# Third expert layer: the three low-rank products of a hidden bank stacked into one of 96 rows, and the first chunk's whole-rank products placed ahead of the low-rank inputs

## The chip, the cores and the metric

The kernel runs on one core of one Trainium2 chip. The metric is the device time of one execution in microseconds; lower is better. Three runs of a kernel give its median.

## The reference, cut to what matters

The model is four pairs of a cross-attention layer and an expert layer over 2048 tokens (8 batches of 256) of 256 features. Only the third expert layer is touched. It is one shared network of 1024 hidden units plus, for each token, a low-rank term of the one expert that the token's gate ranks first:

```
gate   = softmax(y @ gate_W.T + gate_b)           # 8 experts
chosen = one_hot(argmax(gate))                    # one expert a token
u      = y @ lora_A.T, kept for the chosen expert # 8 experts x 4 ranks = 32 columns
hidden = relu(y @ wi.T + wi_b + u @ lora_B)       # 1024 hidden units
x      = x + tanh(g) * (hidden @ wo.T + wo_b)     # y is the normalised x
```

## The kernel before, in words

Everything is one program with one instruction list an engine. The layers follow each other, with all engines meeting at their borders. In the third expert layer (function `experts`, and `choose_low_rank` for the gate) the hidden units are two units of 512 (index `u`), and the tokens four chunks of 512 (index `c`).

Each operand of a product is split into a high part (a rounding copy on ScalarE, helper `high`) and a low part (the rest, a subtraction on VectorE, helper `low`). A product of two operands is then three products on TensorE: high by high, high by low, low by high.

The function `first(u, c)` on TensorE makes the hidden numbers of a chunk in four PSUM banks of 128 hidden units by 512 tokens. For each bank it issues nine products of 512 columns: six whole-rank ones (two halves of the 256 features, three terms each, over 128 partitions) and three low-rank ones over 32 partitions (`lbh` by `uh`, `lbh` by `ul`, `lbl` by `uh`). ScalarE then reads each finished bank twice with the bias and the relu (a whole copy, L1380, and a rounded one, L1381) and counts the semaphore `activated`; VectorE makes the low part (L1386, `f_hl`). The function `second(u, c)` multiplies back in 48 products of 256 columns (L1339), and VectorE adds the four results to the residual (L1412). `run_ahead` sets the order on TensorE and VectorE: `first(0, 0)`, and then `first` of the next chunk always ahead of `second` of this one.

Before all this the low-rank inputs are made. VectorE computes the gate's softmax and the first largest (L1023 to L1045), masks the 32 low-rank columns (`um`, L1238), TensorE turns them chunk by chunk (`turn_inputs`, L1303, two PSUM banks by turns), ScalarE copies each turned chunk twice (`ust` whole and `uh` rounded), VectorE subtracts (`ul`). All four chunks are turned before TensorE's first `first(0, 0)`. The program order of ScalarE and VectorE in this prologue is written out by hand at the ends of `scalar` and `vector`; the main loop of ScalarE comes behind all casts of inputs and weights. A later bank of a chunk waits for the same bank of the chunk before to be read out:

```python
pe.wait_ge(sems["activated"], g * HC + m + 1)
```

The count starts at four, so the first chunk waits for nothing there and bank `m` of the second chunk waits for ScalarE's second reading of bank `m` of the first.

Of the kernel before, what the change touches and what calls it, by code (L numbers as in the profile page):

```python
# [938 lines left out]
def ffn_layer(env, scope, n, following, front):  # L939
# [8 lines left out]
    if routed:  # L948
        t["xn_all"] = front["xn_all"]
        t["gates"] = sb("gates", [P, TILES, cfg["experts"]])  # L950
        t["rows"] = sb("rows", [P, 2 * TILES], I32)
        t["chosen_gates"] = sb("chosen_gates", [P, 2, TILES])
        t["block_expert"] = sb("block_expert", [P, BLOCKS], I32)
    else:
        t["xh"], t["xl"] = (env["homes"][cfg["name"], k] for k in ("xh", "xl"))
        t["uh"] = sb("uh", [32, TOKENS], F32R)
        t["ul"] = sb("ul", [32, TOKENS], F32R)
# [51 lines left out]
class Choice:  # L1009
# [21 lines left out]
    def softmax_rows(self, dve, step, dst):  # L1031
        nc = self.nc
        self.shift(dve, step)
# [182 lines left out]
def choose_low_rank(env, scope, n, t):  # L1216
# [10 lines left out]
    um = t["um"] = sb("um", [P, TILES, 32])  # L1227
# [5 lines left out]
    def vector(dve):  # L1233
        step = Step(dve, sems["chain"])
        choose.softmax_rows(dve, step, choose.c)
        choose.first_largest(step, choose.oh1, choose.c)
        with_r = [P, TILES, E, cfg["lora"]]
        nc.vector.tensor_tensor(um[:].rearrange("p t (e r) -> p t e r", r=cfg["lora"]),  # L1238
                                t["front"]["low_rank"][:].rearrange("p t (e r) -> p t e r", r=cfg["lora"]),
                                choose.oh1[:].unsqueeze(3).to_broadcast(with_r), ALU.mult).then_inc(sems["masked"], 1)  # L1240
# [4 lines left out]
def experts(env, scope, n, t):  # L1245
# [5 lines left out]
    xT, xh, xl, uh, ul = front["xT"], t["xh"], t["xl"], t["uh"], t["ul"]  # L1251
# [13 lines left out]
    lb = sb("lb", [32, U, UNIT])  # L1265
    lbh, lbl = sb("lbh", [32, U, UNIT], F32R), sb("lbl", [32, U, UNIT], F32R)
    ust = sb("ust", [32, 2, 512])
# [6 lines left out]
    u_ps = lambda k: psum[0:32, 4 + k % 2, :]  # L1274
    chunk = lambda c: slice(c * CHUNK, (c + 1) * CHUNK)

    def run_ahead(first, second):
        first(0, 0)
# [8 lines left out]
    def sync(sp):  # L1287
        sp.dma_start(lb[:], dram[f"{name}_lb"]).then_inc(sems["lora_in"], 16)
# [7 lines left out]
    def tensor(pe):  # L1296
        def turn_inputs(k):
# [4 lines left out]
            for q in range(4):  # L1302
                last = nc.tensor.transpose(u_ps(k)[:, q * P:(q + 1) * P], t["um"][:, 4 * k + q, :], ident[:])  # L1303
            last.then_inc(sems["u_turned"], 1)

        def first(u, c):
            g = u * CHUNKS + c
            if c == 0:
                pe.wait_ge(sems["w1_low"], u + 1)
            if u == 0:  # L1310
                pe.wait_ge(sems["x_low"], c + 1)
            tok = chunk(c)
            for m in range(HC):
                pe.wait_ge(sems["activated"], g * HC + m + 1)
                cols = slice(m * P, (m + 1) * P)
                terms = [(w[u][:, k, cols], v[:, k, tok]) for k in range(DC)
                         for w, v in ((w1h, xh), (w1h, xl), (w1l, xh))]
                terms += [(w[:, u, cols], v[:, tok]) for w, v in ((lbh, uh), (lbh, ul), (lbl, uh))]
                for j, (w, v) in enumerate(terms):
                    if m == 0 and u == 0 and j == 3 * DC:  # L1320
                        pe.wait_ge(sems["lora_low"], 1)
                        pe.wait_ge(sems["u_low"], c + 1)
                    last = nc.tensor.matmul(hid_ps[m], w, v, start=(j == 0), stop=(j == len(terms) - 1))
                last.then_inc(sems["hidden"], 1)
# [17 lines left out]
        for k in range(CHUNKS):  # L1342
            turn_inputs(k)
        run_ahead(first, second)

    def scalar(act):
# [10 lines left out]
        high(w1h[0][:], w1raw[0][:], "w1_high")  # L1357
        t["exponentials"](act)
        high(xh[:, :, chunk(0)], xT[:, :, chunk(0)], "x_high")
        act.wait_ge(sems["lora_in"], 16)  # L1360
        high(lbh[:], lb[:], "lora_high")
        high(xh[:, :, chunk(1)], xT[:, :, chunk(1)], "x_high")
        inputs_out(0)
        inputs_out(1)
        high(w2h[0][:], w2raw[0][:], "w2_high")
        inputs_out(2)
        inputs_out(3)
        high(xh[:, :, chunk(2)], xT[:, :, chunk(2)], "x_high")
# [15 lines left out]
    def vector(dve):  # L1384
# [7 lines left out]
        def inputs_low(k):  # L1392
            dve.wait_ge(sems["u_high"], k + 1)
            low(ul[:, chunk(k)], ust[:, k % 2, :], uh[:, chunk(k)], "u_low")
# [23 lines left out]
        weight_lows(0, 1)  # L1418
        x_low(0)
        dve.wait_ge(sems["lora_high"], 1)  # L1420
        low(lbl[:], lb[:], lbh[:], "lora_low")
        inputs_low(0)
        x_low(1)
        inputs_low(1)
        weight_lows(0, 2)
        inputs_low(2)
        inputs_low(3)
        x_low(2)
# [5 lines left out]
        run_ahead(first, second)  # L1434
# [15 lines left out]
    t.update(operands_left=operands_left, banks_left=banks_left, stated=stated, rows_places=rows_places)  # L1450
# [1422 lines left out]
```

## Time and profile before

| what | value |
|---|---|
| median of three runs | 2000.96 us |
| the runs | 2010.17, 2000.35, 2000.96 us |
| span of the profiled execution | 2007.2 us |
| TensorE busy in the span | 1773.6 us (88%) |
| VectorE, ScalarE, GpSimd busy | 1262.0, 975.4, 528.7 us |
| mean granted TensorE clock | 0.929 of full speed |

The span runs from the first to the last instruction of the profiled execution. Its own time has no row beside its span; of the three timed runs the one of 2010.17 us is nearest to it, 3 us above the span, and the median is 6 us below the span. The profile's busy time of TensorE counts overlapping products, so what a product costs in a stream is read from the distance between two starts, not from its duration. In the rows a tile's buffer number and layer number are left out (`f_w1h_home` is either unit's), times are microseconds from the start of the span, and a releaser stands behind `<-`. A granted clock of 1.00 is 2.4 GHz and 0.50 is 1.2 GHz.

### The profile page before, as it was taken

What the parts mean: (1) busy time and instruction counts of PE and PEld (TensorE: products, weight loads), DVE (VectorE), ACT (ScalarE), POOL (GpSimd) and SP (SyncE); (2) the same over time, 40 slices, a digit from 0 to 9 for tenths busy, and PEclk for the clock granted to TensorE, in tenths of its full rate; (3) what the DMA queues carried; (4) which work ended last, traced back from release to release, by engine and by line L of the source; (5) the groups of instructions that cost most, each with busy time, mean ns of one, the idle gap of its engine ahead of it and who ended that gap; (6) DMA issues with size and microseconds to landing.
All of it is one profiled execution on the core that took longest, in us unless ns stands there. A gap on an engine that the chain in (4) does not pass through costs nothing. (4 is left out here: it accounts for less than half of the span.)

```text
span 2007.2 us, 32563 instructions
## 1 busy us (share of the span) xinstructions
PE 1773.6 (88%) x11808; PEld 1447.6 (72%) x11808; DVE 1262.0 (63%) x2310; ACT 975.4 (49%) x1739; POOL 528.7 (26%) x492
## 2 busy tenths in 40 slices
PE   6998899967799996699999969998899789798895
PEld 4667799922577775699999558886577566688884
DVE  6886488546245553588887566765434688656643
ACT  4652476413687671377776234443433255317730
POOL 2220343254333341222220630002000144213333
PEclk9998799988799996699999979999699899899997
DMA  3003377420100000567775220000000100026742
GB/s 109 17 17 126 121 255 248 132 61 0 49 1 12 6 12 25 203 225 229 246 238 169 81 102 1 1 1 1 22 1 1 57 12 12 30 79 208 235 127 81
DMA packets 97139, 178.32 MB, mean 89 GB/s; under 512 B 25184, under 2 KB 61946, under 8 KB 95914
## 3 DMA queue, kind: packets, MB, share of 16 engines
q1 hardware_dynamic: 85496, 146.00, 22.0%
q0 software_dynamic: 11232, 30.69, 5.2%
q8 instruction: 76, 1.25, 0.3%
q14 instruction: 47, 0.39, 0.1%
q10 hardware_dynamic: 288, 0.00, 0.0%
HBM read 149.38 MB, written 27.26 MB: 88 GB/s over the span
## 5 line engine op out<-in xcount | busy, mean ns | idle before, releaser
L1667 POOL DMA_INDIRECT f_block_rows_home<-normed_x,f_token_of_sb x138 | 168.3, 1220 | 451.4 <-PE psum L1713 324.5
L1693 PE MATMUL psum<-f_block_h_sb,f_w1h_home 128*128 128x256 f32 x736 | 211.4, 287 | 30.2 <-issue 10.7
L1693 PE MATMUL psum<-f_block_l_sb,f_w1h_home 128*128 128x256 f32 x736 | 206.8, 281 | 0.0
L1693 PE MATMUL psum<-f_block_h_sb,f_w1l_home 128*128 128x256 f32 x736 | 206.7, 281 | 0.0
L2316 PE MATMUL psum<-a_xT_home,context_w 128*128 128x256 f32 x704 | 182.2, 405 | 13.6 <-PEq L122 9.7
L1703 PE MATMUL psum<-f_w2h_home,f_hidden_h_home 128*128 128x256 f32 x644 | 187.4, 291 | 2.0 <-DVE f_hidden_l_home L1887 1.0
L1703 PE MATMUL psum<-f_w2h_home,f_hidden_l_home 128*128 128x256 f32 x644 | 181.7, 282 | 0.0
L1703 PE MATMUL psum<-f_w2l_home,f_hidden_h_home 128*128 128x256 f32 x644 | 181.7, 282 | 0.0
L1693 PEld LDWEIGHTS psum<-f_block_h_sb,f_w1h_home 128*128 128x128 f32 x736 | 140.8, 191 | 38.5 <-issue 28.6
L2316 PEld LDWEIGHTS psum<-a_xT_home,context_w 128*128 128x128 f32 x704 | 132.6, 198 | 45.3 <-issue 20.0
L2481 ACT ACTIVATE a_probsT_sb<-psum 77x1024 f32<-77x1024 f32 (+1 forms) x128 | 130.7, 1021 | 69.0 <-PE psum L2368 66.5
L1795 ACT ACTIVATE f_hidden_sb<-psum,f_b_sb 128x256 f32<-128x256 f32 x276 | 115.7, 471 | 77.4 <-PE psum L1693 74.6
L2368 PE MATMUL psum<-identity,a_probs_sb 128*77 128x128 f32 (+1 forms) x1024 | 140.4, 278 | 11.0 <-DVE a_inv_sb L2656 8.9
L2408 PE MATMUL psum<-a_wo_sb,a_attT_sb 128*128 128x256 f32 x640 | 147.2, 386 | 2.6 <-ACT a_attT_sb L2503 1.4
L2368 PEld LDWEIGHTS psum<-identity,a_probs_sb 128*77 128x77 f32 (+1 forms) x1024 | 114.8, 141 | 46.0 <-DVE a_inv_sb L2656 19.7
L1693 PEld LDWEIGHTS psum<-f_block_l_sb,f_w1h_home 128*128 128x128 f32 x736 | 141.0, 192 | 0.0
L1693 PEld LDWEIGHTS psum<-f_block_h_sb,f_w1l_home 128*128 128x128 f32 x736 | 140.7, 191 | 0.0
L2408 PEld LDWEIGHTS psum<-a_wo_sb,a_attT_sb 128*128 128x128 f32 x640 | 121.5, 194 | 20.1 <-ACT a_attT_sb L2503 2.7
L1680 POOL DMA_INDIRECT f_w_sb<-sorted_y,f_rows x96 | 93.1, 970 | 141.0 <-DMA sorted_y<-f_result_sb 94.7
L1703 PEld LDWEIGHTS psum<-f_w2h_home,f_hidden_h_home 128*128 128x128 f32 x644 | 122.8, 191 | 2.9 <-DVE f_hidden_l_home L1887 2.7
L1703 PEld LDWEIGHTS psum<-f_w2l_home,f_hidden_h_home 128*128 128x128 f32 x644 | 123.0, 191 | 0.0
L1703 PEld LDWEIGHTS psum<-f_w2h_home,f_hidden_l_home 128*128 128x128 f32 x644 | 122.8, 191 | 0.0
(314 smaller groups left out, 3986.6 us busy)
## 6 DMA issues: line engine op xcount, KB each, us to landing
f_w_sb<-in_f_w SPq DMA_DIRECT2D x161, 512.0 KB
sorted_y<-f_result_sb SPq DMA_DIRECT2D x69, 256.0 KB
normed_x<-f_xn_all SPq DMA_DIRECT2D x24, 256.0 KB, 2.1
f_b_row_sb<-in_f_b SPq DMA_DIRECT2D x46, 128.0 KB
f_w_sb<-in_f_w SPq DMA_DIRECT2D x23, 256.0 KB
f_block_rows_home<-normed_x,f_token_of_sb POOLq DMA_INDIRECT x138
residual<-in_x SPq DMA_DIRECT2D x8, 256.0 KB, 6.2
context_w<-in_a_wk SPq DMA_DIRECT2D x2, 1024.0 KB, 5.0
```

The lines of the kernel that those rows point to most:

```text
L1667: nc.gpsimd.indirect_dma_start(block_rows[b % 2][:, h, :], None, xs, bass.IndirectOffsetOnAxis(ap=column, axis=0)).then_inc(sems[f"rows_in ...
L1680: nc.gpsimd.indirect_dma_start(gathered[j % RING], None, ys, bass.IndirectOffsetOnAxis(ap=t["rows"][:, col:col + 1], axis=0)).then_inc(sem ...
L1693: last = nc.tensor.matmul(hid_ps(q)[:, m, :], w, rhs, start=(j == 0), stop=(j == len(parts) - 1))
L1703: last = nc.tensor.matmul(y_ps[h], v, w, start=(begin and j == 0), stop=(end and j == len(parts) - 1))
L1795: nc.scalar.activation(hidden[q][:, m, :], hid_ps(q)[:, m, :], func, bias=bias[:, 0, m:m + 1]).then_inc(sems["hidden_out"], 1)
L2316: last = nc.tensor.matmul(bank[:, s * SEQ:(s + 1) * SEQ], w[:, k, c * P:(c + 1) * P], xT[:, k, b * SEQ:(b + 1) * SEQ], start=(k == 0), sto ...
L2368: last = nc.tensor.transpose(psum[0:keys, 4 + part, h * P:(h + 1) * P], probs[g % 2][:, 4 * part + h, :], ident[:])
L2408: last = nc.tensor.matmul(bank[:, tile * D:(tile + 1) * D], attT[:, c, tile * P:(tile + 1) * P], wo[:, c, :], start=(c == 0), stop=(c == N ...
L2481: nc.scalar.activation(probsT[h % 2][:, :, tile * P:(tile + 1) * P].rearrange("p (a h) k -> p a h k", a=2), psum[0:keys, 4:6, :].rearrange ...
```

## The change

It does three things. The low-rank operands are stacked in partitions: `um` is written three times side by side (96 columns), so that the turned chunk has the same 32 rows three times; ScalarE rounds all 96 (`u3`), VectorE replaces rows 32 to 63 by the low part. The other factor is loaded three times (`lb`, 96 partitions), rounded (`lb3`), and rows 64 to 95 replaced by the low part. One product of 96 rows then sums the same three terms. Second, TensorE issues the 24 whole-rank products of the first chunk (four banks) ahead of the turning, then turns two chunks, adds the first chunk's four low-rank products, and turns the other two. Third, VectorE makes the low parts of the first unit's weights and of the first chunk (`beside`) between the softmax's shift and its rest, and the orders of ScalarE and VectorE behind that are rewritten to match. Cut to its core:

```diff
-    um = t["um"] = sb("um", [P, TILES, 32])
+    um = t["um"] = sb("um", [P, TILES, 3, 32])
...
     def vector(dve):
         step = Step(dve, sems["chain"])
-        choose.softmax_rows(dve, step, choose.c)
+        choose.shift(dve, step)
+        t["beside"](dve)
+        choose.softmax_rest(dve, step, choose.c)
         choose.first_largest(step, choose.oh1, choose.c)
...
+        nc.vector.tensor_copy(um[:, :, 1:3, :], um[:, :, 0:1, :].to_broadcast([P, TILES, 2, 32])).then_inc(
+            sems["masked"], 1)
...
-        sp.dma_start(lb[:], dram[f"{name}_lb"]).then_inc(sems["lora_in"], 16)
+        for part in range(3):
+            sp.dma_start(lb[part * 32:(part + 1) * 32, :, :], dram[f"{name}_lb"]).then_inc(sems["lora_in"], 16)
...
+            pe.wait_ge(sems["activated"], g * HC + m + 1)
...
+        def low_rank(u, c, m):
+            if m == 0 and u == 0:
+                pe.wait_ge(sems["lora_low"], 1)
+                pe.wait_ge(sems["u_low"], c + 1)
+            nc.tensor.matmul(hid_ps[m], lb3[:, u, m * P:(m + 1) * P], u3[:, chunk(c)], start=False,
+                             stop=True).then_inc(sems["hidden"], 1)
+
+        def begin():
+            for m in range(HC):
+                whole_rank(0, 0, m)
+            turn_inputs(0)
+            turn_inputs(1)
+            for m in range(HC):
+                low_rank(0, 0, m)
+            turn_inputs(2)
+            turn_inputs(3)
+
         def first(u, c):
...
-                terms += [(w[:, u, cols], v[:, tok]) for w, v in ((lbh, uh), (lbh, ul), (lbl, uh))]
...
+                whole_rank(u, c, m)
+                low_rank(u, c, m)
...
         def inputs_out(k):
             act.wait_ge(sems["u_turned"], k + 1)
-            if k >= 2:
-                act.wait_ge(sems["u_low"], k - 1)
-            nc.scalar.activation(ust[:, k % 2, :], u_ps(k), ACT.Copy)
-            high(uh[:, chunk(k)], u_ps(k), "u_high")
+            high(u3[:, chunk(k)], u_ps(k), "u_high")
...
+            low(u3[32:64, chunk(k)], u_ps(k)[32:64, :], u3[32:64, chunk(k)], "u_low")
...
+    def beside(dve):
+        for wanted, out, whole, part, sem in (("w1_high", w1l[0][:], w1raw[0][:], w1h[0][:], "w1_low"),
+                                              ("x_high", xl[:, :, chunk(0)], xT[:, :, chunk(0)], xh[:, :, chunk(0)],
+                                               "x_low")):
```

Three places in the order of the instructions. The first is TensorE at the start of the third expert layer. `f_um_sb` are the masked low-rank columns, `f_x` the tokens, `f_w1` the weights, `f_uh`, `f_ul`, `f_lbh`, `f_lbl` the parts of the low-rank operands. Before:

```order
L1303 MATMUL psum<-identity,f_um_sb 32x128 x16
L1323 MATMUL psum<-f_xh_home,f_w1h_home 128x512
L1323 MATMUL psum<-f_xl_home,f_w1h_home 128x512
L1323 MATMUL psum<-f_xh_home,f_w1l_home 128x512
L1323 MATMUL psum<-f_xh_home,f_w1h_home 128x512
L1323 MATMUL psum<-f_xl_home,f_w1h_home 128x512
L1323 MATMUL psum<-f_xh_home,f_w1l_home 128x512
L1323 MATMUL psum<-f_uh,f_lbh_sb 128x512
L1323 MATMUL psum<-f_ul,f_lbh_sb 128x512
L1323 MATMUL psum<-f_uh,f_lbl_sb 128x512
```

With the change 24 of the whole-rank products stand first, of which the last is the first row here (`f_u` and `f_lb_sb` are `u3` and `lb3`):

```order
L1324 MATMUL psum<-f_xh_home,f_w1l_home 128x512
L1308 MATMUL psum<-identity,f_um_sb 96x128 x8
L1330 MATMUL psum<-f_u,f_lb_sb 128x512 x4
L1308 MATMUL psum<-identity,f_um_sb 96x128 x8
L1324 MATMUL psum<-f_xh_home,f_w1h_home 128x512
L1324 MATMUL psum<-f_xl_home,f_w1h_home 128x512
L1324 MATMUL psum<-f_xh_home,f_w1l_home 128x512
L1324 MATMUL psum<-f_xh_home,f_w1h_home 128x512
L1324 MATMUL psum<-f_xl_home,f_w1h_home 128x512
L1324 MATMUL psum<-f_xh_home,f_w1l_home 128x512
L1330 MATMUL psum<-f_u,f_lb_sb 128x512
```

The turning moved behind the first chunk's whole-rank products and was parted in two, and nine products a bank became seven.

The second place is VectorE at the same border. `f_ra_sb` is the shifted logits, `f_rexp_sb` their exponentials. Before:

```order
L1024 TENSOR_TENSOR f_ra_sb<-f_logits,f_m_sb 128x128
L1035 TENSOR_REDUCE f_m_sb<-f_rexp_sb 128x16
L1036 RECIPROCAL f_m_sb<-f_m_sb 128x16
L1037 TENSOR_TENSOR f_rc_sb<-f_rexp_sb,f_m_sb 128x128
L1041 TENSOR_REDUCE f_m_sb<-f_rc_sb 128x16
L1042 TENSOR_TENSOR f_oh_sb<-f_rc_sb,f_m_sb 128x128
```

Now:

```order
L1023 TENSOR_TENSOR f_ra_sb<-f_logits,f_m_sb 128x128
L1456 TENSOR_TENSOR f_w1l_home<-f_w1raw,f_w1h_home 128x1024
L1456 TENSOR_TENSOR f_xl_home<-f_xT_home,f_xh_home 128x2x512
L1037 TENSOR_REDUCE f_m_sb<-f_rexp_sb 128x16
L1038 RECIPROCAL f_m_sb<-f_m_sb 128x16
```

The two low parts that the first whole-rank product needs moved from behind the mask to ahead of the softmax's rest.

The third place is ScalarE in the prologue, up to its main loop. `f_w2h` are the weights of the way back. Before:

```order
L1354 ACTIVATE f_ust_sb<-psum 32x512
L1348 ACTIVATE f_uh<-psum 32x512
L1354 ACTIVATE f_ust_sb<-psum 32x512
L1348 ACTIVATE f_uh<-psum 32x512
L1348 ACTIVATE f_xh_home<-f_xT_home 128x2x512 x2
L1348 ACTIVATE f_w1h_home<-f_w1raw 128x1024
L1348 ACTIVATE f_w2h_sb<-f_w2raw 128x1024
L1380 ACTIVATE f_h_sb<-psum,f_b_sb 128x512
```

Now:

```order
L1368 ACTIVATE f_w2h_home<-f_w2raw 128x1024
L1368 ACTIVATE f_u<-psum 96x512 x2
L1368 ACTIVATE f_xh_home<-f_xT_home 128x2x512
L1368 ACTIVATE f_u<-psum 96x512 x2
L1368 ACTIVATE f_xh_home<-f_xT_home 128x2x512
L1368 ACTIVATE f_w1h_home<-f_w1raw 128x1024
L1368 ACTIVATE f_w2h_sb<-f_w2raw 128x1024
L1397 ACTIVATE f_h_sb<-psum,f_b_sb 128x512
```

The reading of a turned chunk is one copy instead of two; the casts of the last chunk and of the second unit's weights (three) still stand between the last turned chunk and the main loop.

## Rows read from the trace of the kernel before

**Rows 1.** The page's part 1, busy time by engine over the span.

```profile
PE 1773.6 (88%) x11808; PEld 1447.6 (72%) x11808; DVE 1262.0 (63%) x2310; ACT 975.4 (49%) x1739; POOL 528.7 (26%) x492
```

**Rows 2.** Stretches: length, busy us (instructions) by engine, PEclk, DMA share, GB/s.

```profile
1453.00:1558.00 105.00, 104.98 (x601) 82.12 (x600) 38.10 (x71) 31.66 (x50) 0.00 (x0) 1.00 0.00 1
```

**Rows 3.** Timeline of TensorE, one hidden bank: start, duration, engine, line, operation.

```profile
1443.10 0.50 PE L1323 MATMUL psum<-f_xh_home,f_w1h_home 128*128 128x512 f32 x1
1443.43 0.40 PE L1323 MATMUL psum<-f_xl_home,f_w1h_home 128*128 128x512 f32 x1
...
1444.35 0.39 PE L1323 MATMUL psum<-f_xh_home,f_w1l_home 128*128 128x512 f32 x1
1444.67 0.49 PE L1323 MATMUL psum<-f_uh,f_lbh_sb 32*128 32x512 f32 x1
1445.00 0.39 PE L1323 MATMUL psum<-f_ul,f_lbh_sb 32*128 32x512 f32 x1
...
1445.56 0.50 PE L1323 MATMUL psum<-f_xh_home,f_w1h_home 128*128 128x512 f32 x1
```

**Rows 4.** Timeline of TensorE, borders of `second(0, 0)`.

```profile
1452.96 0.38 PE L1339 MATMUL psum<-f_w2h_home,f_hh_sb 128*128 128x256 f32 x1
1453.18 0.28 PE L1339 MATMUL psum<-f_w2l_sb,f_hh_sb 128*128 128x256 f32 x1
...
1458.73 0.40 PE L1323 MATMUL psum<-f_xh_home,f_w1h_home 128*128 128x512 f32 x1
1458.96 0.40 PE L1323 MATMUL psum<-f_xl_home,f_w1h_home 128*128 128x512 f32 x1
```

**Rows 5.** Timeline of TensorE in the second expert layer, products over 78 partitions.

```profile
488.91 3.60 PE L569 MATMUL psum<-context_w,f_spare 128*77 128x512 f32 x8
492.35 0.72 PE L590 MATMUL psum<-identity,f_xn_all 78*128 78x78 f32 x8
492.90 1.88 PE L521 MATMUL psum<-context_w,f_spare 128*77 128x512 f32 x4
```

**Rows 6.** Timeline of VectorE, the layer's prologue.

```profile
1419.97 0.28 DVE L1035 TENSOR_REDUCE f_m_sb<-f_rexp_sb 128x16 f32<-128x128 f32 x1 [0.54 <-ACT f_rexp_sb L1029]
...
1423.13 1.22 DVE L1386 TENSOR_TENSOR f_w1l_home<-f_w1raw,f_w1h_home 128x1024 fp32r<-128x1024 f32 x1
...
1426.54 0.67 DVE L1386 TENSOR_TENSOR f_ul<-f_ust_sb,f_uh 32x512 fp32r<-32x512 f32 x1
```

**Rows 7.** Timeline of ScalarE, the layer's prologue and the first bank's reading.

```profile
1418.68 1.06 ACT L1348 ACTIVATE f_w1h_home<-f_w1raw 128x1024 fp32r<-128x1024 f32 x1 [4.05 <-PEq L122]
...
1430.57 0.57 ACT L1348 ACTIVATE f_uh<-psum 32x512 fp32r<-32x512 f32 x1
1431.04 1.99 ACT L1348 ACTIVATE f_xh_home<-f_xT_home 128x1024 fp32r<-128x1024 f32 x2
...
1434.83 0.66 ACT L1380 ACTIVATE f_h_sb<-psum,f_b_sb 128x512 f32<-128x512 f32 x1
```

**Rows 8.** Timeline of TensorE, the layer's prologue.

```profile
1423.27 1.89 PE L1303 MATMUL psum<-identity,f_um_sb 128*32 128x128 f32 x8 [6.01 <-DVE f_um_sb L1238]
...
1429.69 0.78 PE L1323 MATMUL psum<-f_xh_home,f_w1h_home 128*128 128x512 f32 x1
...
1430.69 0.63 PE L1323 MATMUL psum<-f_xh_home,f_w1l_home 128*128 128x512 f32 x1
1431.12 0.63 PE L1323 MATMUL psum<-f_xh_home,f_w1h_home 128*128 128x512 f32 x1
```

**Rows 9.** Stretches, with columns as in group 2, around changes of the granted clock.

```profile
1590.60:1596.10 5.50, 0.00 (x0) 0.00 (x0) 2.57 (x5) 1.57 (x4) 0.00 (x0) 0.87 0.78 207
1596.10:1602.00 5.90, 5.88 (x18) 3.56 (x19) 3.82 (x5) 0.72 (x1) 2.41 (x3) 0.54 0.37 147
1437.00:1438.00 1.00, 1.00 (x4) 0.69 (x3) 0.54 (x1) 0.00 (x0) 0.00 (x0) 0.67 0.00 0
```

**Rows 10.** Issues of transfers in the prologue: size, median us from issue to landing.

```profile
f_lb_sb<-in_f_lb SPq DMA_DIRECT2D x1, 128.0 KB, 2.4
```

More of the change, by code:

```diff
@@ L1273, in experts, with run_ahead @@
     y_ps = [psum[:, 4 + q, 0:D] for q in range(4)]
-    u_ps = lambda k: psum[0:32, 4 + k % 2, :]
+    u_ps = lambda k: psum[0:96, 4 + k % 2, :]
     chunk = lambda c: slice(c * CHUNK, (c + 1) * CHUNK)
-    def run_ahead(first, second):
-        first(0, 0)
+    def run_ahead(begin, first, second):
+        begin()
         for u in range(U):
@@ L1302, in turn_inputs @@
             for q in range(4):
-                last = nc.tensor.transpose(u_ps(k)[:, q * P:(q + 1) * P], t["um"][:, 4 * k + q, :], ident[:])
+                last = nc.tensor.transpose(u_ps(k)[:, q * P:(q + 1) * P],
+                                           t["um"][:, 4 * k + q, :, :].rearrange("p j r -> p (j r)"), ident[:])
             last.then_inc(sems["u_turned"], 1)
-        def first(u, c):
[L1307 to L1312, printed above, removed]
-            for m in range(HC):
[L1314 to L1317, printed above, removed]
-                terms += [(w[:, u, cols], v[:, tok]) for w, v in ((lbh, uh), (lbh, ul), (lbl, uh))]
[L1319 to L1324, printed above, removed]
@@ new lines, in whole_rank @@
+        def whole_rank(u, c, m):
+            g = u * CHUNKS + c
+            if m == 0:
+                if c == 0:
+                    pe.wait_ge(sems["w1_low"], u + 1)
+                if u == 0:
+                    pe.wait_ge(sems["x_low"], c + 1)
+            pe.wait_ge(sems["activated"], g * HC + m + 1)
+            cols = slice(m * P, (m + 1) * P)
+            terms = [(w[u][:, k, cols], v[:, k, chunk(c)]) for k in range(DC)
+                     for w, v in ((w1h, xh), (w1h, xl), (w1l, xh))]
+            for j, (w, v) in enumerate(terms):
+                nc.tensor.matmul(hid_ps[m], w, v, start=(j == 0), stop=False)
@@ L1340, in second @@
                 last.then_inc(sems["product"], 1)
-        for k in range(CHUNKS):
-            turn_inputs(k)
-        run_ahead(first, second)
+        run_ahead(begin, first, second)
     def scalar(act):
@@ L1416, in second @@
                     nc.vector.bn_stats(env["stats"][:, tile, :], x[:, tile, :]).then_inc(sems["stated"], 1)
-        weight_lows(0, 1)
-        x_low(0)
         dve.wait_ge(sems["lora_high"], 1)
-        low(lbl[:], lb[:], lbh[:], "lora_low")
+        low(lb3[64:96], lb[64:96], lb3[64:96], "lora_low")
+        x_low(1)
+        weight_lows(0, 2)
         inputs_low(0)
-        x_low(1)
         inputs_low(1)
-        weight_lows(0, 2)
+        x_low(2)
         inputs_low(2)
         inputs_low(3)
-        x_low(2)
         x_low(3)
@@ L1433, in vector @@
         dve.wait_ge(sems["w2_low"], U)
-        run_ahead(first, second)
+        run_ahead(lambda: first(0, 0), first, second)
+    def beside(dve):
+        for wanted, out, whole, part, sem in (("w1_high", w1l[0][:], w1raw[0][:], w1h[0][:], "w1_low"),
+                                              ("x_high", xl[:, :, chunk(0)], xT[:, :, chunk(0)], xh[:, :, chunk(0)],
+                                               "x_low")):
+            dve.wait_ge(sems[wanted], 1)
+            nc.vector.tensor_tensor(out, whole, part.bitcast(F32), ALU.subtract).then_inc(sems[sem], 1)
     def operands_left(engine):
```

32 lines of the change are left out of this document (15 added, 17 removed).

## The prediction

> **What bounds the kernel now.** I read the page's busy times first: TensorE is busy 88% of the span [rows 1]. That is a mean over stages, so I cut out the one that changes. From 1453 to 1558 us, the main part of the third expert layer, TensorE is busy 104.98 of 105.00 us at a granted clock of 1.00, while VectorE works 38.10 and ScalarE 31.66 us [rows 2]. There the layer is as long as its products, and what is taken from TensorE comes off the time until another engine needs more. Ahead of it lies a prologue from the layer's border (ScalarE's first cast starts at 1418.68 [rows 7]) to 1429.69 us, when the first whole-rank product starts [rows 8], in which TensorE mostly waits, and two chunks that run partly at half clock. What follows the layer (the next attention's query weights on SP, its keys on TensorE) waits for the last product by the code, so a gain here should reach the end. Then I read the timeline of the three engines, start by start.
>
> **The products.** A hidden bank takes 1445.56 - 1443.10 = 2.46 us for nine products [rows 3]. Between products of 128 rows the starts are 0.23 us apart (1458.73 to 1458.96) [rows 4]. Nine of these would be 2.07, not 2.46: the first product of the bank takes 0.33, the last of 128 rows 0.32 (1444.35 to 1444.67), the first of 32 rows 0.33, and the other two together 0.56 instead of 0.46 [rows 3]. So each change between 128 and 32 rows costs about 0.1 us on both its sides, some 0.4 us a bank. Two products go, and with them 2 x 0.23 = 0.46 us.
>
> What a product of 96 rows takes, and whether it is such a change, no row shows. The bounds are 0.23 us with no border, as of 128 rows, and 0.23 + 0.4, as of 32 rows. The nearest rows are products of 78 rows between such of 128: eight of them take 492.90 - 492.35 = 0.55 us, and the eight products before them 492.35 - 488.91 = 3.44, 0.43 each, just as the four behind them (1.88 with the last one's tail) [rows 5]. Two borders of 0.2 us would leave 0.15 us for eight products. I therefore take 0.23 and no border: seven products, 1.61 us, 0.85 less a bank. The Trainium skill's page "TensorEngine Tiling (Array Packing)", section Tiling Modes, knows heights of 128, 64 and 32 rows and says that a change of mode drains the array. By it 96 rows need the full height and drain nothing, which gives the same sum; the borders of 32 rows in this trace agree with it, and 96 rows themselves no row here shows.
>
> From `second(0, 0)` on (1452.96 us) there remain six calls of `first` behind a `second`, whose first product has no border even now (0.23 at 1458.73): 6 x (4 x 0.85 - 0.10) = 19.8 us. Seven calls of `second` stand behind a `first`, and their first product takes 0.22 (1452.96 to 1453.18) where the mean of 48 is 5.77 / 48 = 0.12 [rows 4]: 7 x 0.10 = 0.7. **Main part: 20.5 us less.** ScalarE reads a bank in two steps of 0.66 [rows 7], 1.3 us against TensorE's 1.61, so it does not become the bound; VectorE needs less.
>
> **The prologue.** ScalarE's first cast ends at 1418.68 + 1.06 = 1419.74 and the next, now that of the first chunk, about 0.95 us later (four casts take 1434.83 - 1431.04 = 3.79) [rows 7]. VectorE makes the first low part from 1419.8 on and the second by about 1422.1 (1.22 us each, a little overlapped) [rows 6]. So TensorE starts its products at about 1422.2 instead of 1429.69.
>
> Its clock is then at half: products are 0.43 apart (1430.69 to 1431.12) [rows 8]. When it comes back I take from two restarts. In the prologue of before, a clock of 0.67 in the microsecond from 1437 puts the rise at 1437.7, 8.0 us after 1429.69 [rows 8, 9]. After the hole that ends at 1596.1 a mean of 0.54 over 5.90 us puts it 5.4 us after the restart [rows 9]. The first stretch was broken up by products of 32 rows, so I take 5.4 and keep 8.0 as the bound. In 5.4 us 12.6 of the 24 products are done; 11.4 x 0.23 = 2.6 us remain, and the 24 end at 1422.2 + 8.0 = 1430.2, called E (1431.4 with the late clock).
>
> Behind E stands a chain that runs from engine to engine. Eight turned pieces took 1.89 us at half clock [rows 8]; at full clock I take half, so four are read from E + 0.6. ScalarE's copy 0.57 [rows 7], VectorE's low part 0.67 [rows 6], and the first low-rank product starts at E + 2.0. Four of 0.23 end at E + 2.9, eight more turned pieces at E + 4.0, ScalarE's last copy at E + 4.6. **There the new stall begins.** ScalarE has three casts left (0.95 each) before its main loop, then the first bank's two readings (2 x 0.66): the bank is free at E + 8.75. TensorE, with nothing left since E + 4.0, waits for it with the second chunk's first product. Before, those casts lay beside a first bank at half clock that ended as they did: the main loop began at 1434.83 [rows 7], and the first bank's nine products ended at about 1429.69 + 9 x 0.43 + 0.4 = 1434.0. So the second chunk starts at 1438.9, idle for 4.7 us ahead of that.
>
> Does the clock survive the idle time? After 5.50 us without a product (1590.6 to 1596.1) the mean clock was 0.87, so it fell some 4 us into the hole; it then stayed low for 5.4 us of work, which lost 2.7 us [rows 9]. Here TensorE has 4.7 us of nothing behind 4 us of sparse work. I take the fall and its 2.7 us; the bounds are nothing, and 4.0 (8.0 us at half). The second chunk's four banks take 4 x 1.61 + 2.7 = 9.1 us, and `second(0, 0)` starts at 1448.1 where it started at 1452.96: **4.9 us less.**
>
> **Edits at no cost.** The copy that triples the mask has no row; between 0.67 and 1.22 us (512 and 1024 elements on VectorE [rows 6]) it ends with the softmax's rest (1419.97 to 1423.13, 3.2 us [rows 6]) at about 1426.5, under the 24 products that end at 1430.2. Past that, it would cost its whole length. Three loads of the low-rank factor: one lands in 2.4 us [rows 10]; even one after the other they are in at 1425.8, and the three casts behind them on ScalarE end at 1429, ahead of the first turned chunk at E + 0.6. On SP's queue the bias and the next attention's loads go two issues later; the bias is read from 1437 on and the others after the last product. ScalarE's four dropped copies (0.57 each) were not what TensorE waits for now. Of the added wait in `beside`, behind it on VectorE stands the softmax's rest, covered by the same 24 products.
>
> **Sum.** 20.5 + 4.9 = 25.4 us. The trace is of an execution of span 2007.2 us; the median lies 6 us below that, but the layer's rows are the same work, so I take the difference from the median of 2000.96: **1975.6 us**. About 0.5%, 10 us, is what a measurement of this kernel can tell from no change; the three runs themselves spread by that.
>
> **The rivals.**
> - *The clock survives.* The hole is 4.7 us and the fall was seen some 4 us into one. Then the 2.7 us stay: 1972.9.
> - *The clock is late both times.* 8.0 us at half in the first chunk (1.2 more) and 8.0 us behind the hole (1.3 more): 1978.1. The prologue of before speaks for it; the other restart against.
> - *96 rows keep their borders.* Then a bank saves the two products alone, 0.46: 24 x 0.46 = 11.0, and the second chunk 1.6 and the first 0.4 less: 11.0 + 2.9 = 13.9, or 1987.1. The 78-row products speak against [rows 5]. This is also the way in which the change would not do what it says. By the Trainium skill's page "TensorEngine Tiling (Array Packing)", section Tiling Modes, it would not happen.
> - *Slower: the clock stays down behind the hole.* At half clock the rest of the layer, 6.4 + 105.0 - 20.5 = 90.9 us of work, takes twice that: 1972.9 + 90.9 = 2063.8. Each microsecond at half loses 0.5, so from 56 us on the gain is gone, and from 76 on the kernel is slower by over 0.5%. For it speaks that 8 us of dense products did not raise the clock at once; against it that it rose in both restarts [rows 9] and then held for 105 us [rows 2].
>
> **Chances.** Forecast 0.62 (1974 to 1977 by itself), clock survives 0.14, late clock 0.10, borders 0.09, slower 0.02, and 0.03 for a mishap that I don't see. The range takes the first three and, for the spread of the runs shown on either side, goes from 1968 to 1984; it leaves out the borders and the rest. Faster by over 0.5% are all cases but the last two: 0.94; the rest is 0.04 within and 0.02 slower.
>
> **What would show it.** In the new profile: products at about 1422 us; low-rank products of 96 rows 0.23 us from their neighbours, a bank of 1.61 us and a `first` and `second` together of about 12.1 instead of 15.5; TensorE idle for some 4.7 us before the second chunk, released by ScalarE's second reading (the line of `activated`); the clock at 0.50 for about 5 us behind it. A bank of 2.0 us means borders. No hole, or one released by another engine, means that the chain behind E is wrong.

## The result and the profile after

| | before | after |
|---|---|---|
| median | 2005.57 us (2000.35 to 2012.97, 4 runs) | 1981.19 us (1978.98 to 1988.19, 4 runs) |
| span of the profiled execution (its own time) | 2007.2 us | 1977.2 us (1978.98 us) |
| TensorE busy | 1773.6 us | 1744.6 us |

The ratio after to before is 0.9882, 95% interval 0.9848 to 0.9915: faster by 24.4 us of medians, where 25.4 was forecast. The forecast time of 1975.6 us lies 5.6 below the median measured now, because one more run of before (2012.97) raised its median by 4.6.

The busy times of the page's part 1 after, to be held against [rows 1]:

```profile
PE 1744.6 (88%) x11744; PEld 1441.1 (73%) x11744; DVE 1262.1 (64%) x2311; ACT 972.8 (49%) x1735; POOL 528.8 (27%) x492
```

TensorE is busy 29.0 us less with 64 products less; the others hardly changed. To place that I measure the layer from VectorE's first reduction behind the border to the first product of the next attention's keys; times "behind the border" are counted from that reduction. Of the kernel before, from the timelines of VectorE and TensorE:

```profile
1418.82 0.29 DVE L1023 TENSOR_REDUCE f_m_sb<-f_logits 128x16 f32<-128x128 f32 x1 [1.21 <-PEq L122]
...
1558.60 0.76 PE L512 MATMUL psum<-ctx_features,context_w 128*128 128x308 f32 x2 [0.62 <-issue]
```

And after:

```profile
1416.98 0.29 DVE L1022 TENSOR_REDUCE f_m_sb<-f_logits 128x16 f32<-128x128 f32 x1 [1.21 <-PEq L122]
...
1531.47 0.76 PE L512 MATMUL psum<-ctx_features,context_w 128*128 128x308 f32 x2 [0.63 <-issue]
```

The layer took 139.78 us and takes 114.49: 25.29 less. The spans differ by 30.0; the border lies 1.84 earlier and the stretch behind the layer is 2.9 shorter (448.6 to 445.7). Neither can be put down to the change: in a second profile of the same changed kernel (below) the border came 2.06 later than in the first and the stretch behind was 4.2 longer, and the layer took 113.21.

**The main part.** TensorE's timeline of one hidden bank after, to be held against [rows 3]:

```profile
1443.13 0.40 PE L1324 MATMUL psum<-f_xh_home,f_w1h_home 128*128 128x512 f32 x1
1443.36 0.40 PE L1324 MATMUL psum<-f_xl_home,f_w1h_home 128*128 128x512 f32 x1
...
1444.29 0.40 PE L1324 MATMUL psum<-f_xh_home,f_w1l_home 128*128 128x512 f32 x1
1444.52 0.40 PE L1330 MATMUL psum<-f_u,f_lb_sb 96*128 96x512 f32 x1
1444.76 0.40 PE L1324 MATMUL psum<-f_xh_home,f_w1h_home 128*128 128x512 f32 x1
```

The 96-row product starts 0.23 us behind its neighbour and the next starts 0.24 behind it; the 0.33 of [rows 3] are gone on both sides. The bank takes 1444.76 - 1443.13 = 1.63 us. The borders of `second`, to be held against [rows 4]:

```profile
1446.39 0.28 PE L1361 MATMUL psum<-f_w2h_home,f_hh_sb 128*128 128x256 f32 x1
1446.52 0.28 PE L1361 MATMUL psum<-f_w2l_sb,f_hh_sb 128*128 128x256 f32 x1
...
1458.53 0.28 PE L1361 MATMUL psum<-f_w2h_home,f_hh_sb 128*128 128x256 f32 x1
```

The first product of `second` takes 0.13 instead of 0.22, and `first` and `second` together 12.14 instead of 15.5. From `second(0, 0)` to the keys it is 1531.47 - 1446.39 = 85.08 us where it was 105.64: 20.56 less. TensorE is still the bound there: in the view by stretches (length, busy us and instructions of PE, PEld, DVE, ACT, POOL, then the granted clock) it is busy for 83.84 of 84.00 us of the main part, at full clock, as in [rows 2]:

```profile
1447.00:1531.00 84.00, 83.84 (x549) 76.48 (x547) 38.31 (x72) 31.23 (x50) 0.00 (x0) 1.00 0.00 1
```

**The prologue.** TensorE's timeline after, to be held against [rows 8]:

```profile
1420.39 0.77 PE L1324 MATMUL psum<-f_xh_home,f_w1h_home 128*128 128x512 f32 x1 [4.97 <-DVE f_xl_home L1456]
...
1425.22 0.60 PE L1324 MATMUL psum<-f_xh_home,f_w1l_home 128*128 128x512 f32 x1
1425.64 0.41 PE L1324 MATMUL psum<-f_xh_home,f_w1h_home 128*128 128x512 f32 x1
1425.89 0.40 PE L1324 MATMUL psum<-f_xl_home,f_w1h_home 128*128 128x512 f32 x1
...
1428.40 1.03 PE L1308 MATMUL psum<-identity,f_um_sb 128*96 128x128 f32 x8
1430.49 1.17 PE L1330 MATMUL psum<-f_u,f_lb_sb 96*128 96x512 f32 x4 [1.06 <-DVE f_u L1403]
1431.50 1.04 PE L1308 MATMUL psum<-identity,f_um_sb 128*96 128x128 f32 x8
1437.34 0.76 PE L1324 MATMUL psum<-f_xh_home,f_w1h_home 128*128 128x512 f32 x1 [4.80 <-ACT f_hh_sb L1398]
```

The first product starts 3.41 us behind the border instead of 10.87. The distance between starts is 0.42 up to 1425.64 and 0.25 behind it, so the clock came back 5.3 us after the start. Then comes the hole of 4.80 us, released by ScalarE's second reading. What ScalarE does in it, to be held against [rows 7]:

```profile
1429.04 1.08 ACT L1368 ACTIVATE f_u<-psum 96x512 fp32r<-96x512 f32 x2 [5.90 <-PE psum L1308]
...
1432.14 1.08 ACT L1368 ACTIVATE f_u<-psum 96x512 fp32r<-96x512 f32 x2 [1.08 <-PE psum L1308]
1433.11 1.05 ACT L1368 ACTIVATE f_xh_home<-f_xT_home 128x1024 fp32r<-128x1024 f32 x1
1434.06 1.05 ACT L1368 ACTIVATE f_w1h_home<-f_w1raw 128x1024 fp32r<-128x1024 f32 x1
1435.00 1.05 ACT L1368 ACTIVATE f_w2h_sb<-f_w2raw 128x1024 fp32r<-128x1024 f32 x1
1435.95 0.67 ACT L1397 ACTIVATE f_h_sb<-psum,f_b_sb 128x512 f32<-128x512 f32 x1
1436.52 0.68 ACT L1398 ACTIVATE f_hh_sb<-psum,f_b_sb 128x512 fp32r<-128x512 f32 x1
```

Three casts, then the two readings, in one unbroken row up to 1437.2; and ahead of the first turned chunk ScalarE had stood idle for 5.90 us. Behind the hole the granted clock is at half for 5.3 us, by the view by stretches:

```profile
1437.34:1442.60 5.26, 5.26 (x13) 4.10 (x13) 3.58 (x6) 4.57 (x8) 0.00 (x0) 0.50 0.00 0
1442.89:1446.39 3.50, 3.50 (x16) 2.83 (x15) 0.82 (x2) 2.53 (x4) 0.00 (x0) 1.00 0.02 5
```

So `second(0, 0)` starts 29.41 us behind the border instead of 34.14: 4.73 less.

### The profile page after: what moved, and what is told of

The parts are those of the page before. It is cut to its first block and busy times, and to the rows that moved or that the text cites. A ratio compares the mean times of both kernels' runs of the same rounds, so it can differ in the third digit from the quotient of the medians.

```text
span 1977.2 us, 32432 instructions
## 1 busy us (share of the span) xinstructions
PE 1744.6 (88%) x11744; PEld 1441.1 (73%) x11744; DVE 1262.1 (64%) x2311; ACT 972.8 (49%) x1735; POOL 528.8 (27%) x492
## 5 line engine op out<-in xcount | busy, mean ns | idle before, releaser
L2430 PEld LDWEIGHTS psum<-a_wo_sb,a_attT_sb 128*128 128x128 f32 x640 | 120.2, 192 | 19.6 <-ACT a_attT_sb L2525 2.7
```

The costliest lines, as they stand in the source:

```text
L2430: last = nc.tensor.matmul(bank[:, tile * D:(tile + 1) * D], attT[:, c, tile * P:(tile + 1) * P], wo[:, c, :], start=(c == 0), stop=(c == N ...
```

## The experiments

Ten kernels ran: the changed kernel once more, and nine edits of it, two of these twice. The questions: what of the bank's 0.85 us is two products and what is borders, and which heights have a border; what in the prologue makes the gain; and what the hole is made of. "Layer" is the time defined above, `second` the start of `second(0, 0)` behind the border, "period" the distance between the second and the third start of `second` in chunk order, that is one `first` and one `second` at full clock.

| kernel | median us (runs) | ratio to before, 95% | layer | `second` | period |
|---|---|---|---|---|---|
| before (profile above) | | | 139.78 | 34.14 | 15.54 |
| changed | 1981.19 (4) | 0.9882 [0.9848, 0.9915] | 114.49 | 29.41 | 12.12 |
| changed, again | 1983.94 (5) | 0.9867 [0.9843, 0.9891] | 113.21 | 28.16 | 12.12 |
| one product, 32 rows | 1999.51 (1) | | 131.39 | 34.76 | 13.68 |
| the same, again | 2000.92 (4) | 0.9962 [0.9944, 0.998] | 130.30 | 34.04 | 13.68 |
| one product, 64 rows | 1986.81 (1) | | 124.49 | 29.90 | 13.68 |
| three products, 96 rows | 1993.92 (1) | | 128.56 | 32.43 | 13.97 |
| three products, 32 rows | 2015.31 (12) | 1.0029 [1.0014, 1.0043] | 141.17 | 35.52 | 15.53 |
| filler | 1975.48 (1) | | 111.08 | 26.04 | 12.11 |
| turned first | 1984.20 (6) | 0.9874 [0.985, 0.9899] | 112.37 | 27.32 | 12.12 |
| early casts | 1982.09 (4) | 0.9866 [0.985, 0.9882] | 110.72 | 25.67 | 12.12 |
| early casts and readings | 1977.64 (5) | 0.9848 [0.9822, 0.9874] | 106.50 | 21.46 | 12.11 |
| and early turning | 1978.11 (5) | 0.9836 [0.981, 0.9863] | 105.95 | 20.82 | 12.11 |
| the same, again | 1975.80 (5) | 0.9841 [0.9826, 0.9857] | 106.47 | 21.32 | 12.12 |

The kernel before, run beside them, had medians of 2008.06, 2008.29 and 2008.18 us in these comparisons.

### Rows and products apart

```diff
-            nc.tensor.matmul(hid_ps[m], lb3[:, u, m * P:(m + 1) * P], u3[:, chunk(c)], start=False,
+            nc.tensor.matmul(hid_ps[m], lb3[0:32, u, m * P:(m + 1) * P], u3[0:32, chunk(c)], start=False,
```

> The changed kernel with the low-rank product of each bank over the first 32 partitions alone (high by high; the two low terms are left out). Theory H (what cost was the change of height: about 0.1 us on each side of a border between 128 and 32 rows): one product of 32 rows costs its 0.23 and both borders, so a bank takes about 2.0 us where the changed kernel's takes 1.62, and the stretch from second(0, 0) to the last product grows from 85 us by 24 x 0.4, to about 95. Rival C (products over 32 rows are dear one by one, 1.1 / 3 = 0.37 us each, and no border costs anything): a bank of 1.75 us, a stretch of 88.

The second kernel has `0:64` in both places.

> The changed kernel with the low-rank product over the first 64 partitions alone (the low-weight by high-input term is left out). If heights of 64 are a mode of their own, as the list of modes on the Trainium skill's page TensorEngine Tiling (Array Packing), section Tiling Modes, has it, a bank takes about 2.0 us, as with 32 rows under theory H. If only a quarter height is drained, 1.62 us, as with 96 rows.

The other two issue the product three times a bank, over `0:96` and over `0:32`:

```diff
-            nc.tensor.matmul(hid_ps[m], lb3[:, u, m * P:(m + 1) * P], u3[:, chunk(c)], start=False,
-                             stop=True).then_inc(sems["hidden"], 1)
+            for j in range(3):
+                last = nc.tensor.matmul(hid_ps[m], lb3[0:96, u, m * P:(m + 1) * P], u3[0:96, chunk(c)], start=False,
+                                        stop=(j == 2))
+            last.then_inc(sems["hidden"], 1)
```

> The changed kernel with the 96-row low-rank product issued three times a bank (the low-rank term is then counted three times). Theory H: two products of 0.23 us more and no border, a bank of 1.62 + 0.46 = 2.08 us, a stretch from second(0, 0) to the last product of 85 + 24 x 0.46 = 96 us. Rival C does not say otherwise for full height; a bank of 2.46 us, as before the change, would mean that it was neither the height nor the count but the place of these products at the end of a bank.

> The changed kernel with three 32-row products a bank instead of the one of 96 rows (high by high three times, the low terms left out), so the new order without what the stacking saves on TensorE. Theories S and H: a bank of 2.46 us again, the stretch from second(0, 0) to the last product 105 to 106 us as before; second(0, 0) at about 32 to 33 us behind the border; 1 to 2 us less than before the change in all, ratio 0.999 to 1.000. Rival O: 5 us less, ratio 0.9975.

The periods make a table of two by two. With one product instead of three: 15.53 - 13.68 = 1.85 for 32 rows and 13.97 - 12.12 = 1.85 for 96, over eight products: 0.23 each. With 96 rows instead of 32: 15.53 - 13.97 = 1.56 and 13.68 - 12.12 = 1.56, over four banks: 0.39 a bank. The two add up without a remainder. Theory H holds, and rival C, which has no borders, does not: with one 32-row product a bank takes 1.62 + 0.39 = 2.01 us, not 1.75. The 64-row product costs what the 32-row one does. Its bank in TensorE's timeline:

```profile
1441.95 0.40 PE L1324 MATMUL psum<-f_xh_home,f_w1l_home 128*128 128x512 f32 x1
1442.28 0.50 PE L1330 MATMUL psum<-f_u,f_lb_sb 64*128 64x512 f32 x1
1442.71 0.50 PE L1324 MATMUL psum<-f_xh_home,f_w1h_home 128*128 128x512 f32 x1
1443.04 0.39 PE L1324 MATMUL psum<-f_xl_home,f_w1h_home 128*128 128x512 f32 x1
```

Starts 0.33, 0.43 and 0.33 apart instead of three times 0.23: the border of [rows 3] on both sides, 0.4 in all. Behind three products of 96 rows, in that kernel's timeline, there is none:

```profile
1440.97 0.39 PE L1324 MATMUL psum<-f_xh_home,f_w1l_home 128*128 128x512 f32 x1
1441.20 0.86 PE L1331 MATMUL psum<-f_u,f_lb_sb 96*128 96x512 f32 x3
1441.90 0.28 PE L1363 MATMUL psum<-f_w2h_home,f_hh_sb 128*128 128x256 f32 x1
```

0.23 to the first and 0.70 for three. By the Trainium skill's page "TensorEngine Tiling (Array Packing)", section Tiling Modes, there are heights of 128, 64 and 32 rows and a change among them drains the array; the borders at 64 and 32 rows agree with it, and 96 rows run here as full height does.

Three products of 32 rows in the new order undo on TensorE what the stacking saves (the turned 96 rows, the three loads and the new orders stay), and the main part is back (141.17 - 35.52 = 105.65 us against 105.64). Its layer is 1.4 us longer than before, the median run 0.29% longer than before. The profile is of an execution of 2010.74 us, 4.6 below that kernel's median, so what the median run lost beyond the 1.4 was not seen.

The expectation of 1 to 2 us less was missed: `second(0, 0)` starts at 35.52, not at 32 to 33. TensorE's timeline ahead of its hole, and the stretch from 1426.00 to the hole's end, show where the rest went:

```profile
1427.70 4.43 PE L1331 MATMUL psum<-f_u,f_lb_sb 32*128 32x512 f32 x12 [1.05 <-DVE f_u L1405]
1432.06 1.94 PE L1308 MATMUL psum<-identity,f_um_sb 128*96 128x128 f32 x8
1426.00:1438.76 12.76, 6.95 (x27) 4.84 (x25) 7.03 (x8) 7.34 (x11) 0.00 (x0) 0.61 0.00 0
```

A mean clock of 0.61 over 12.76 us is half clock for the last 10 of them, so the clock fell at about 1428.8, among the twelve 32-row products and 5.2 us ahead of the hole (1434.00 to 1438.76). The twelve products take 4.36 us (12 x 0.23 is 2.8) and the turning behind them 1.94, where the changed kernel's takes 1.04: some 2.5 us together, as much as was missed. So the 1.4 us hold for these products in this order; without that fall the order alone would have been worth about 1 us, an estimate from these rows. **To within some 2 us the stacking is the whole gain; the new order without it brought none.**

### The clock with products of 32 rows

The one-product kernel of 32 rows stood out: its layer was not some 10 us over the changed kernel's, as with 64 rows, but 17. It ran again.

> The single product of 32 rows once more: it sums the high-by-high term alone and leaves the two low terms out. A bank of 2.00 us as with 64 rows. In the first run the granted clock stayed at half for 18.7 us behind the hole and the layer took 131.4. Theory chance: this differs from run to run; with a return after about 5 us the layer takes 124 to 125, as with 64 rows. Theory rows: products of 32 rows with 128-row neighbours delay the return each time, and the layer is 131 again.

It came out at 130.30. Of the two executions profiled, the stretches behind the hole and where the clock came back; first run:

```profile
1436.54:1450.83 14.29, 14.29 (x28) 8.39 (x29) 5.09 (x8) 7.10 (x12) 0.00 (x0) 0.50 0.01 1
1450.83:1455.20 4.37, 4.37 (x21) 4.37 (x21) 1.17 (x2) 1.27 (x2) 0.00 (x0) 0.50 0.01 2
1455.30:1457.00 1.70, 1.70 (x16) 1.70 (x16) 0.49 (x1) 0.00 (x0) 0.00 (x0) 0.96 0.00 0
```

Second run:

```profile
1440.41:1454.69 14.28, 14.28 (x28) 8.38 (x28) 5.10 (x8) 7.09 (x12) 0.00 (x0) 0.50 0.00 1
1454.69:1459.00 4.31, 4.31 (x23) 4.31 (x23) 1.18 (x2) 1.26 (x2) 0.00 (x0) 0.57 0.01 2
```

Through all four banks with a 32-row product the clock stayed at 0.50, and it came back some 4 us into `second(0, 0)`, 18 to 19 us behind the hole, both times. With 64 rows it came back 4.5 us behind it, with three products of 32 rows a bank 3.8 us behind it (from the mean clocks of 0.57 over the first 5.29 us and 0.55 over 4.24). Two executions out of two speak against chance for the single 32-row product, and so do the four timed runs of the repeat: they lie 15 to 20 us above the changed kernel's median beside them, where the layer is 17 us longer and a return as with 64 rows would make some 11. But "32 rows delay it" doesn't hold in general either. What decides stays open.

### What the hole is made of

```diff
             turn_inputs(3)
+            for j in range(19):
+                nc.tensor.matmul(psum[:, 6, :], w1h[0][:, 0, 0:P], xh[:, 0, chunk(0)], start=True, stop=True)
```

> The changed kernel with 19 more products of 512 columns (into a bank that nothing reads) behind the last turned chunk, where TensorE now has nothing for 4.8 us; the result is the same. Theory G (the clock falls because TensorE has nothing there, and the second chunk pays for it): the second chunk still starts some 20.4 us behind the layer's border, but at full clock: its four banks take 6.5 us instead of 9.05, and second(0, 0) starts 2.5 us earlier, at about 26.9 us behind the border instead of 29.4. Rival: the clock is low there for another reason (the restart itself, the turning): four banks of 9 us, no change.

The filler's products lie in the hole and go to a bank that nobody reads. TensorE's timeline:

```profile
1428.83 4.60 PE L1343 MATMUL psum<-f_xh_home,f_w1h_home 128*128 128x512 f32 x19
1433.88 0.47 PE L1324 MATMUL psum<-f_xh_home,f_w1h_home 128*128 128x512 f32 x1 [0.45 <-ACT f_hh_sb L1400]
```

The four banks behind, by the view by stretches:

```profile
1433.88:1440.43 6.55, 6.55 (x29) 5.36 (x30) 4.40 (x7) 6.55 (x12) 0.00 (x0) 1.00 0.01 3
```

The second chunk starts as late as without them (19.49 us behind the border, 19.56 and 20.36 in the changed kernel) but at full clock at once, and `second(0, 0)` follows after 6.55 us instead of 9.05 or 8.60. That is the clock's part: 2.1 to 2.5 us here.

The other way is to shorten the hole. The three casts, and that of the third chunk, which stood between the turned chunks, go ahead of the turned chunks on ScalarE, into its idle 5.9 us:

```diff
         inputs_out(0)
         inputs_out(1)
-        high(xh[:, :, chunk(2)], xT[:, :, chunk(2)], "x_high")
         inputs_out(2)
         inputs_out(3)
-        high(xh[:, :, chunk(3)], xT[:, :, chunk(3)], "x_high")
-        high(w1h[1][:], w1raw[1][:], "w1_high")
-        high(w2h[1][:], w2raw[1][:], "w2_high")
```

(the four removed lines stand ahead of `inputs_out(0)` now).

> Only the three casts go ahead of the first turned chunk on ScalarE, into its idle 5.9 us. Theory casts: the hole of 4.8 us before the second chunk shrinks by their 2.85 to about 1.9 us, released by the second reading as now; if the clock holds over such a hole, second(0, 0) starts 5.5 us earlier than in the changed kernel (at 23.9 us from the border) and the layer takes 109.0; if the clock falls all the same, 2.85 earlier (26.6) and 111.6. Rival: the hole is set by the readings and the turned chunks alone; then it stays 4.8 and the layer 114.5.

TensorE's first product behind the hole, and the stretches from there on:

```profile
1437.89 0.47 PE L1324 MATMUL psum<-f_xh_home,f_w1h_home 128*128 128x512 f32 x1 [1.97 <-ACT f_hh_sb L1398]
1437.89:1439.30 1.41, 1.41 (x6) 1.19 (x7) 1.41 (x2) 1.41 (x3) 0.00 (x0) 0.99 0.00 0
1439.42:1442.40 2.98, 2.98 (x8) 2.30 (x7) 2.88 (x5) 2.32 (x5) 0.00 (x0) 0.50 0.00 0
```

The hole is 1.97 us as the casts' theory said, released by the same reading. The clock did not fall in it, but behind it: the first six products run at full clock, then it falls at about 1439.3 for some 3 us of work, which costs about half of that. `second(0, 0)` lies between the two figures expected (25.67 between 23.9 and 26.6). The layer is 2.5 to 3.8 us shorter than the changed kernel's; the timed runs don't resolve that (0.9866 beside 0.9867).

### The order on TensorE, and a better one

```diff
-            for m in range(HC):
-                whole_rank(0, 0, m)
-            turn_inputs(0)
-            turn_inputs(1)
-            for m in range(HC):
-                low_rank(0, 0, m)
-            turn_inputs(2)
-            turn_inputs(3)
+            for k in range(CHUNKS):
+                turn_inputs(k)
+            first(0, 0)
```

> The changed kernel with all four chunks turned ahead of the first whole-rank product, as before the change; the stacking stays. Theory S (the stacking is worth all, the order nothing: what the earlier start wins is given back in the hole of 4.8 us and in a second stretch of low clock): the first product starts about 13 us behind the layer's border instead of 3.4, no hole follows, the clock is low once, and second(0, 0) starts at 28 to 30 us, against 29.4 with the change and 34.1 before; ratio to before 0.987 to 0.989, as the whole change. Rival O (the order is worth the roughly 5 us by which the prologue got shorter): second(0, 0) at 33 to 34 us, ratio about 0.990.

With the stacking kept and the old order on TensorE, the layer takes 112.37 us, 0.8 to 2.1 less than the changed kernel's, and the ratio is the same within its interval. TensorE's first whole-rank product:

```profile
1434.83 0.78 PE L1324 MATMUL psum<-f_xh_home,f_w1h_home 128*128 128x512 f32 x1
...
1437.39 0.40 PE L1330 MATMUL psum<-f_u,f_lb_sb 96*128 96x512 f32 x1
1437.62 0.40 PE L1324 MATMUL psum<-f_xh_home,f_w1h_home 128*128 128x512 f32 x1
```

It starts 13.19 us behind the border, 9.8 later than in the changed kernel, and no hole follows; the clock is back at about 1437.2, within the first bank, and stays. That is 2.3 us behind the first product, where the changed kernel's two profiles had 5.3 and 3.5; half of the difference, 0.6 to 1.5 us, is most of what its layer is shorter by. So the two orders on TensorE are worth the same within what the clock's return scatters: what the new one wins at its start it pays in waiting for the low-rank inputs, in the hole and at the clock behind it.

So by the layer's rows the order is worth something only without the hole (106.50 us against 112.37 in the table). In the next kernel ScalarE makes the three casts first and reads the finished banks of the first chunk ahead of the last two turned chunks (VectorE's low parts of these two follow its work on the first chunk); in the one after, TensorE also turns two chunks ahead of the first chunk's last bank:

```diff
+                if g == 0:
+                    inputs_out(2)
+                    inputs_out(3)
...
-            for m in range(HC):
+            for m in range(HC - 1):
                 whole_rank(0, 0, m)
             turn_inputs(0)
             turn_inputs(1)
+            whole_rank(0, 0, HC - 1)
```

> The changed kernel with ScalarE's four remaining casts ahead of the first turned chunk (ScalarE has nothing to do for 5.9 us there), and the first chunk's four banks read out ahead of the last two turned chunks. Theory G (the hole is ScalarE's list, and the fall of the clock follows from the hole): no hole, no second stretch of low clock, second(0, 0) at about 22 us behind the border instead of 29.4, 7.5 us less than the changed kernel: ratio to before about 0.984. Rival: another wait (a turned chunk, a low part) takes the hole's place: second(0, 0) later than 26 us.

> As the kernel with the casts and readings ahead, and the first two chunks turned ahead of the first chunk's last bank, so that the way over ScalarE and VectorE to the first low-rank product (1.06 us of nothing on TensorE) lies beside six products. Theory G: second(0, 0) at about 21 us behind the border, 8.4 us less than the changed kernel; ratio to before about 0.9835. Rival: the mask is not ready in time and TensorE waits ahead of the turning instead; no gain over the other.

> The changed kernel once more, beside the best variant on one chip. From VectorE's first reduce of the layer to the next attention's keys 114.5 us as before, ratio to the kernel before 0.985 to 0.9915. If the time outside the layer scatters by several us between profiled executions, its span may differ by that while the layer's time stays within 0.2 us.

> The variant with early casts, early readings and early turning, beside the changed kernel. Its layer was 8.5 us shorter (106.0 against 114.5). Theory A: all of it reaches the end, 8.5 us or 0.42% below the changed kernel of this call. Theory B: a part is given back behind the layer, 3 to 4 us below it (0.15 to 0.2%).

TensorE's timeline of the last one, second run:

```profile
1431.96 1.04 PE L1308 MATMUL psum<-identity,f_um_sb 128*96 128x128 f32 x8
1433.02 0.47 PE L1324 MATMUL psum<-f_xh_home,f_w1h_home 128*128 128x512 f32 x1
1433.32 0.39 PE L1324 MATMUL psum<-f_xl_home,f_w1h_home 128*128 128x512 f32 x1
```

No hole and no fall of the clock: the second chunk starts at 14.4 us behind the border where it started at 20.4 and 19.6, at full pace. Reading the banks early brought most of it, as its theory G had it: `second(0, 0)` at 21.46, about 22 expected. The layer is 6.7 to 8.5 us shorter than the changed kernel's. Beside it in one comparison the median is 1975.80 against 1983.94 us, 8.1 less, so theory A (all of it reaches the end) is nearer than theory B; the two ratios, 0.9841 [0.9826, 0.9857] and 0.9867 [0.9843, 0.9891], overlap at their ends, so the size is not settled. Early turning moves `second(0, 0)` by 0.1 to 0.6 us instead of about 1, and the timed runs (1977.64 and 1978.11) don't tell it from the kernel without it. By its layer this is the shortest version that ran. The repeat of the changed kernel missed its expectation: its layer was 1.3 us shorter than in the first profile, not the same within 0.2.

## Why the prediction was right

Step by step, in us behind the border (the prediction's times less 1418.82):

| step | forecast | changed | again |
|---|---|---|---|
| first whole-rank product | 3.4 | 3.41 | 3.42 |
| clock back after it | 5.4 | 5.3 | 3.5 |
| the 24 products end (E) | 11.4 | 11.42 | 10.62 |
| first low-rank product | E + 2.0 | E + 2.09 | E + 2.09 |
| hole | 4.7 | 4.80 | 4.81 |
| second chunk starts | E + 8.75 | E + 8.94 | E + 8.94 |
| clock back after it | 5.4 | 5.3 | 4.4 |
| `second(0, 0)` | 29.3 | 29.41 | 28.16 |
| main part, less | 20.5 | 20.56 | 20.59 |
| prologue, less | 4.9 | 4.73 | 5.98 |

- *The products.* The value taken between the bounds for 96 rows, 0.23 with no border, by the eight 78-row products [rows 5], is what the bank shows. The split into two products (0.46) and borders (0.4) is what the four kernels of rows and products measured, 0.46 and 0.39.
- *The hole.* Its place, its length and its releaser were as forecast; early casts took 2.8 us out of it and left the readings. What the clock costs behind it was 2.1 to 2.5 by the filler, where 2.7 was taken.
- *Edits at no cost.* The copy that triples the mask had no row; it takes 0.69 us, inside the bounds of 0.67 and 1.22, and ends 4.2 us ahead of the end of the 24 products (1428.40):

```profile
1423.48 0.69 DVE L1245 COPY f_um_sb<-f_um_sb 128x1024 f32<-128x1024 f32 x1
```

  The three loads made ScalarE wait 1.15 us, ahead of its idle 5.9.
- *The clock's return.* Between two profiles of one kernel it differed by 1.8 us in the first chunk and 0.9 in the second, and half of these 2.7 together is what their layers differ by (114.49 and 113.21). That the first profile hit the 5.4 both times to about 0.1 us is therefore luck, and so is the agreement of the layer's 25.29 with 25.4; by the second profile it is 26.57. Of the kernel before there is one profile, with a late return (8.0 us), so the prologue's gain is not known better than to 1 or 2 us. The late bound of 8.0 us, from the prologue of before, wasn't reached. The rival on the slower side, a clock that stays down, did not happen here, though 18 to 19 us with one 32-row product a bank show that it can be far longer than the bound.
- *What the prediction didn't say.* It gave the prologue's 4.9 us as one sum and never took the two parts of the change by themselves. The runs do, for TensorE: with the old order there and the rest of the change `second(0, 0)` starts 6.8 us earlier than before (27.32), with the new order and three 32-row products 1.4 later (35.52). The new orders of VectorE and ScalarE are in both; no run takes them out by themselves. The 7.5 us by which the products start earlier are more than spent by the new order: the hole takes 4.8, the wait for the first low-rank product 1.06, the turning, which now stands between the products, 2.1, and half clock lasts 10.6 us in all where it lasted 8.0, which costs 1.3: 9.3 together. The rest of the prologue's 4.7 is then 6.5 us of shorter banks in the first two chunks, by difference; eight banks at 0.85 are 6.8.
- *The base.* The one figure that was off is the median of before that the difference was taken from, 2000.96 of three runs; with more runs it is 2005.6 to 2008.3. The difference of medians is off by 1.0 us, the time by 5.6; the 95% interval of the ratio allows 17 to 30 us, so it is the layer's rows and not the timed runs that confirm the terms.

## What to carry to other kernels

A product over few partitions that stands between full ones can cost more by its borders than by itself (0.39 against 0.23 us here), and 96 rows had no border here, so stacking three terms of 32 rows took away the borders and two of the three products; look in the trace for starts that are further apart on either side of such a product. Work moved earlier on the busiest engine is worth only what the next engine in the chain lets through: price the hole that it opens and the half clock behind it (4.8 and 2.1 to 2.5 us here), and move the next engine's casts too. Where a change has two parts, work out each by itself, since one can carry the other.

## What the hardware did that was not expected

- A product of 64 rows costs the same border as one of 32 (starts 0.33, 0.43, 0.33), one of 96 none.
- A hole of 1.97 us, with sparse work ahead of it, was followed by a fall of the granted clock, and it came some 1.4 us after the work had begun again (1437.89 to 1439.3). With three 32-row products a bank it came among twelve such products, 5.2 us ahead of the hole. So a fall needs no hole; what decides was not found.
- The clock stayed at 0.50 for 18 to 19 us of unbroken work in the kernel with one 32-row product a bank, twice; in the two profiles of the changed kernel it came back within 3.5 to 5.3 us.
